# Attention passes of a four-layer graph network: VectorE weighs a batch's rows before it scores the next batch

## The chip, the cores and the metric

The kernel runs on one core of a Trainium2 chip. The metric is device time in microseconds (us) of one execution. Engines are called TensorE (PE; its weight loads are PEld), VectorE (DVE), ScalarE (ACT), GpSimd (POOL) and SyncE (SP). Each has its own instruction queue, taken strictly in order; waits are on semaphores.

## The reference, cut to what matters

The network has 6250 nodes with 256 features and 106250 edges, sorted by target node. Four layers follow one another: a convolution over edges, a mean over neighbours, and two attention layers. The change touches the two attention layers only. With the first three lines ahead of both, they compute (second attention layer, cut; the first has an edge term more in the score, and the second also gives each node a loop to itself):

```
h   = maximum(layernorm(x), 0)
xl  = (h @ W).reshape(n, 8, 32)
a_src, a_dst = einsum('nhc,hc->nh', xl, att_src), einsum('nhc,hc->nh', xl, att_dst)
logits = leaky_relu(a_src[src] + a_dst[dst], 0.2)
ex     = exp(logits - segment_max(logits, dst)[dst])
alpha  = ex / segment_sum(ex, dst)[dst]
out    = segment_sum(xl[src] * alpha[:, :, None], dst).reshape(n, 256) + bias
x      = x + layernorm(out) * gamma + beta
```

## The kernel before, in words

The function gat (L1853) makes one attention pass; it is called twice, with the tags g2 and g3. Edges stand in steps of 128 (one per partition), a step never holds edges of two node tiles of 128 nodes, and 16 steps are a batch: 55 batches a pass (NB). Three buffers of gathered rows (rows0 to rows2) take turns. The helper triples (L96) writes the first three batches out, runs a loop of 17 turns with three batches each, and writes the last batch out.

What happens to batch t:

- GpSimd (gather, L1957) issues 16 indirect DMAs that fetch the sender rows of 16 steps. Ahead of gathers 0, 5, 9 and 14 it waits for marks of other engines (dictionary behind): these are for earlier batches, dt, zt, q1, dt.
- SyncE (load, L1935) loads the indices, the target row numbers (bc), the lines, the heads and in g2 the edge scores.
- VectorE makes the transposed one-hot (transpose_hot, L2100, instruction L2103); TensorE uses it to spread the receivers' scores (spread, L1980, signal sp).
- VectorE scores (score, L2106): it waits for all 16 gathers (gas), for sp and for the turn of the batch before (zt), and adds three terms, L2112, L2114 and L2116. The last gives the signal z.
- TensorE turns the scores (turn, L2005, matmul L2008, signal zt). within (L2118), between (L2138), differ (L2168) and rate (L2162) on VectorE find a running maximum per node and the differences; TensorE turns them back (back, L2019, signal dt), and ScalarE takes the exponent into psT (L2075, L2076, signal w).
- VectorE weighs (weigh, L2181, L2187): it waits for w and multiplies the gathered rows of the batch by the weights in place, in two halves, each with a signal msg.
- TensorE sums the messages per node tile (sums, L1988, matmuls L2001 and L1998), in four quarters of four steps. The first and third quarter wait for a half of msg and for the one-hots sel that ScalarE makes (one_hot, L2052). The quarters use two PSUM buffers in turn.
- VectorE adds the sums to the accumulator (add, L2191, L2203 and L2200), a quarter at a time, and rescales one tile (rescale, L2210, L2214), which also waits for w.

The engines run skewed. VectorE's body(t) handles the differences of batch t, adds the four quarters of batch t - 1, rescales, and then did score(t + 1) and weigh(t). TensorE's body(t) is: tiles_of(t + 1), the four quarters of sums for batch t - 1, factors, back(t), spread(t + 1), turn(t + 1). Both engines begin a body with tiles_of (L1975 and L2217; the calls that show are L1976 and L2218): it loads the numbers of the node tiles of a batch from SBUF into the engine's registers, with one TENSOR_LOAD of 16 or 17 values. There is no planner; the order is the order in which the bodies are written.

Of the kernel before, what the change touches and what calls it, by code (L numbers as in the profile page):

```python
# [164 lines left out]
def wide(t):  # L165
    return t.rearrange("p a d -> p (a d)")
# [1686 lines left out]
def gat(nc, k, tag, edge, own, beta):  # L1853
# [14 lines left out]
    with es:  # L1868
# [214 lines left out]
        def _(v):  # L2083
# [8 lines left out]
            def shifted(t):  # L2092

                x = k.x[:, t * G:(t + 1) * G, :]
                nc.vector.tensor_tensor(x, x, beta_row[:, :].unsqueeze(1).broadcast_to([P, G, D]), ALU.add
                                        ).then_inc(S["xb"], 1)
# [3 lines left out]
            def transpose_hot(t, b, i):  # L2100
                v.wait_ge(S["bc"], t * 16 + 16)
                reach(v, S["sp"], t)
                nc.vector.tensor_scalar(oneT[:, :], bc[:, :], k.lane[:, 0:1], None, ALU.is_equal  # L2103
                                        ).then_inc(S["oh"], 1)

            def score(t, b, i):  # L2106
                v.wait_ge(gas[b], i * full + full)
                v.wait_ge(S["sp"], t + 1)
                reach(v, S["zt"], t)
                a_src = rows[b][:, :, 0:TW].rearrange("p u (h c) -> p h u c", c=HW)[:, :, :, CH]  # L2110
                part = psE[:, 0:U * 3 * H].rearrange("p (u q h) -> p q h u", q=3, h=H)
                nc.vector.tensor_tensor(z[:, :, :], a_src, part[:, 0], ALU.add).then_inc(S["v"], 1)  # L2112
                v.wait_ge(S["v"], t * 13 + 1)
                nc.vector.tensor_tensor(z[:, :, :], z[:, :, :], part[:, 1], ALU.add).then_inc(S["v"], 1)  # L2114
                v.wait_ge(S["v"], t * 13 + 2)
                nc.vector.tensor_tensor(z[:, :, :], z[:, :, :], part[:, 2], ALU.add).then_inc(S["z"], 1)  # L2116

            def within(t, b, i):  # L2118
                v.wait_ge(S["zt"], t + 1)
                v.wait_ge(lns[b], i * 16 + 16)  # L2120
                useless = k.mask[:, ds(t, 1)]
                if edge:
                    v.wait_ge(aes[b], i * 16 + 16)
                    nc.vector.scalar_tensor_tensor(out=zz[:, :], in0=psE[:, scores], scalar=useless, in1=ae[b][:, :],
                                                   op0=ALU.add, op1=ALU.add).then_inc(S["v"], 1)
                else:
                    nc.vector.tensor_scalar(zz[:, :], psE[:, scores], useless, None, ALU.add).then_inc(S["v"], 1)
                v.wait_ge(S["v"], t * 13 + 3)
                nc.vector.scalar_tensor_tensor(out=sc[:, :], in0=zz[:, :], scalar=0.2, in1=zz[:, :], op0=ALU.mult,
                                               op1=ALU.max).then_inc(S["v"], 1)  # L2130
                v.wait_ge(S["v"], t * 13 + 4)
                nc.vector.tensor_tensor_scan(fwd[:, :], ln[b][:, pen], sc[:, :], LOW, ALU.add, ALU.max
                                             ).then_inc(S["v"], 1)
                v.wait_ge(S["v"], t * 13 + 5)
                nc.vector.tensor_tensor_scan(loc[:, ::-1], ln[b][:, nextp][:, ::-1], fwd[:, ::-1], LOW, ALU.add, ALU.max
                                             ).then_inc(S["loc"], 1)
# [31 lines left out]
            def differ(t, b, i):  # L2168
                v.wait_ge(S["v"], t * 13 + 12)
                reach(v, S["dt"], t)  # L2170
                nc.vector.scalar_tensor_tensor(out=m1[:, :], in0=ln[b][:, pref], scalar=cf[:, 0:1], in1=loc[:, :],
                                               op0=ALU.add, op1=ALU.max).then_inc(S["v"], 1)
                v.wait_ge(S["v"], t * 13 + 13)
                nc.vector.scalar_tensor_tensor(out=mx[:, :], in0=ln[b][:, suf], scalar=cb[:, 0:1], in1=m1[:, :],
                                               op0=ALU.add, op1=ALU.max).then_inc(S["mx"], 1)
                v.wait_ge(S["mx"], t + 1)
                if own:
                    nc.vector.tensor_tensor(me[:, :], ln[b][:, last], mx[:, :], ALU.mult)
                nc.vector.tensor_tensor(df[:, :], sc[:, :], mx[:, :], ALU.subtract).then_inc(S["d"], 1)

            def weigh(t, b, i):  # L2181
                v.wait_ge(S["w"], t + 1)
                weight = psT[:, turned].rearrange("p (h u) -> p u h", h=H)
                for half in range(2):
                    u = slice(half * (U // 2), (half + 1) * (U // 2))
                    r = rows[b][:, u, 0:TW].rearrange("p u (h c) -> p u h c", c=HW)
                    nc.vector.tensor_tensor(r[:, :, :, 0:CH], r[:, :, :, 0:CH],  # L2187
                                            weight[:, u, :].unsqueeze(3).broadcast_to([P, U // 2, H, CH]), ALU.mult
                                            ).then_inc(S["msg"], 1)

            def add(t, at, q):  # L2191

                summed(v, t, q)
                of = psA[:, q % 2]
                for n in range(Q):
                    u = q * Q + n
                    ready = known(v, t * U + u if u else t + 1)
                    to = wide(k.acc[:, ds(at[u], 1), :])
                    if n == 3:
                        ins = nc.vector.tensor_tensor(to, to, of[:, 2, 0:RW], ALU.add)  # L2200
                    else:
                        to = to.rearrange("p (o d) -> p o d", o=2)
                        ins = nc.vector.tensor_tensor(to, to, of[:, 0:2, n * HALF:(n + 1) * HALF], ALU.add)  # L2203
                    if u:
                        ins._wait_ge(S["acc"], ready)
                    else:
                        ins._wait_ge(S["rs"], ready)
                    ins.then_inc(S["acc"], 1)

            def rescale(t, at):  # L2210
                v.wait_ge(S["w"], t + 1)
                v.wait_ge(S["acc"], t * U)
                to = wide(k.acc[:, ds(at[U], 1), 0:TW]).rearrange("p (h c) -> p h c", c=HW)
                nc.vector.scalar_tensor_tensor(out=to, in0=psT[:, factor].unsqueeze(2).broadcast_to([P, H, HW]),  # L2214
                                               scalar=1.0, in1=to, op0=ALU.add, op1=ALU.mult).then_inc(S["rs"], 1)

            def tiles_of(t):  # L2217
                return nc.values_load_multi_w_load_instructions(  # L2218
                    k.node_of[0:1, ds(t * KP, K)], engines=[DVE], min_val=0, max_val=NT - 1,
                    skip_runtime_bounds_check_because="made in prepare() from counts of at most NT - 1")[1]  # L2220

            def body(t, b, i):
                first = isinstance(t, int) and t == 0
                last_one = isinstance(t, int) and t == NB - 1
                after, more = (b + 1) % 3, i + (b + 1) // 3
                if first:
                    transpose_hot(0, 0, 0)
                    for n in range(5):
                        shifted(n)
                    score(0, 0, 0)  # L2230
                else:
                    at = tiles_of(t - 1)
                    if isinstance(t, int) and t <= 2:
                        shifted(t + 4)
                if not last_one:
                    transpose_hot(t + 1, after, more)
                within(t, b, i)
                if not first:
                    add(t - 1, at, 0)
                between(t, b, i)  # L2240
                if not first:
                    add(t - 1, at, 1)
                differ(t, b, i)
                rate(t, b, i)
                if first:
                    v.sem_inc(S["rs"], 1)
                else:
                    add(t - 1, at, 2)
                    add(t - 1, at, 3)
                    rescale(t, at)  # L2250
                if not last_one:
                    score(t + 1, after, more)
                weigh(t, b, i)

            triples(v, NB, body)
            at = tiles_of(NB - 1)
            for q in range(4):
# [316 lines left out]
```

## Time and profile before

| | us |
|---|---|
| median of 3 runs | 5556.87 (5554.14 to 5564.05) |
| profiled execution | 5560.9 |
| its span | 5559.1 |
| VectorE busy in the span | 4053.2 (73%) |
| TensorE busy | 3861.1 (69%) |
| GpSimd busy | 3637.7 (65%) |
| ScalarE busy | 2944.2 (53%) |

The span is the time from the first to the last recorded instruction. The shares are means over the four layers and what lies between. The attention passes take about 2940 to 4107 us (g2) and 4283 to 5453 us (g3) of the span. "Idle before" an instruction is the time its engine stood still ahead of it, with what ended that; "issue" means that the profile shows nothing that was waited for. The instructions of a queue's sequencer (PEldq, DVEq: register operations, semaphore waits) are not counted as busy. The granted clock is a share of TensorE's full 2.4 GHz.

### The profile page before, as it was taken

Reading aid. Unit: us, or ns where it says so; the run is one execution under the profiler, and the core shown is the slowest. Engines: PE = TensorE matmul, PEld = TensorE weight load, DVE = VectorE, ACT = ScalarE, POOL = GpSimd, SP = SyncE. Lnnn points to the kernel's source line nnn. Section 1 sums busy time; section 2 is a strip of 40 time slices with the busy share of each in tenths; the row PEclk is TensorE's granted clock in tenths of the full one; section 3 lists DMA queues with packets and bytes.
Section 4 is the critical chain, followed back from the end, with each engine's and each line's share of the span. In section 5 each row is a group of like instructions: output and inputs, shape, how many; then the busy total and the mean of one; then the engine's idle time right before and its main releaser. Section 6 shows DMA issues by size and latency. Waiting matters only on the chain. (4 is left out here: it accounts for less than half of the span.)

```text
span 5559.1 us, 88639 instructions
## 1 busy us (share of the span) xinstructions
PE 3861.1 (69%) x21123; PEld 3024.9 (54%) x21124; DVE 4053.2 (73%) x9127; ACT 2944.2 (53%) x8412; POOL 3637.7 (65%) x3635
## 2 busy tenths in 40 slices
PE   4799999999775666666674555555565555665565
PEld 3577777777554555555553455444533445555552
DVE  4799999999773333333376888887876788888888
ACT  4799999999554444444453333333334334333432
POOL 2577777777327777777706777777721777777770
PEclk9999999999877888888786777777787777777777
DMA  8444444444215544555435555555522555554542
GB/s 265 116 97 99 98 99 99 98 99 98 68 60 140 134 134 133 134 134 134 116 121 153 146 146 146 144 143 145 146 87 79 141 140 144 144 144 142 141 138 95
DMA packets 705680, 700.27 MB, mean 126 GB/s; under 512 B 458546, under 2 KB 574063, under 8 KB 703779
## 3 DMA queue, kind: packets, MB, share of 16 engines
q0 software_dynamic: 173552, 491.76, 31.2%
q1 hardware_dynamic: 390663, 177.29, 12.4%
q10 hardware_dynamic: 141372, 30.14, 2.8%
q8 instruction: 39, 0.64, 0.0%
q14 instruction: 54, 0.44, 0.0%
HBM read 634.29 MB, written 64.08 MB: 126 GB/s over the span
## 5 line engine op out<-in xcount | busy, mean ns | idle before, releaser
L1135 POOL DMA_INDIRECT c0rows<-rows,c0idx x872 | 986.6, 1131 | 282.8 <-issue 268.2
L1967 POOL DMA_INDIRECT g2rows<-sender_rows,g2idx x864 | 844.0, 977 | 264.8 <-issue 259.8
L1967 POOL DMA_INDIRECT g3rows<-sender_rows,g3idx x864 | 829.4, 960 | 281.3 <-issue 261.6
L901 POOL DMA_INDIRECT g1rows<-rows,g1idx x872 | 833.5, 956 | 265.7 <-issue 260.5
L1022 DVE TENSOR_TENSOR acc<-acc,g1psA 128x258 f32 x660 | 279.9, 424 | 725.2 <-PE g1psA L927 569.7
L1164 ACT ACTIVATE c0z<-c0rows,c0sh 128x128 f32<-128x128 f32 x2640 | 795.7, 408 | 1.6 <-DVE c0prod L1331 1.6
L930 PE MATMUL g1psA<-g1rows,g1sel 128*128 128x129 f32 x2640 | 475.3, 348 | 360.3 <-DMA g1rows<-rows,g1idx 317.3
L930 PEld LDWEIGHTS g1psA<-g1rows,g1sel 128*128 128x128 f32 x2640 | 456.2, 259 | 403.3 <-issue 339.2
L2001 PE MATMUL g3psA<-g3rows,g3sel 128*128 128x136 f32 x2640 | 444.2, 328 | 156.8 <-DVE g3rows L2187 102.5
L1256 PE MATMUL c0psA<-c0prod,c0sel 128*128 128x256 f32 x1760 | 547.2, 393 | 3.5 <-DVE acc L1345 3.5
L2001 PE MATMUL g2psA<-g2rows,g2sel 128*128 128x132 f32 x2640 | 432.7, 324 | 165.0 <-DVE g2rows L2187 102.4
L2001 PEld LDWEIGHTS g3psA<-g3rows,g3sel 128*128 128x128 f32 x2640 | 412.3, 231 | 231.4 <-issue 113.1
L2001 PEld LDWEIGHTS g2psA<-g2rows,g2sel 128*128 128x128 f32 x2640 | 401.9, 231 | 236.8 <-issue 113.3
L1259 PE MATMUL c0psA<-c0prod,c0sel 128*128 128x192 f32 x1760 | 430.3, 326 | 0.0
L1345 DVE TENSOR_TENSOR acc<-acc,c0psA 128x256 f32 x880 | 367.7, 418 | 24.7 <-PE c0psA L1259 2.1
L955 ACT ACTIVATE g1fT<-g1psF 128x512 f32<-128x512 f32 x104 | 62.1, 597 | 574.9 <-PE g1psA L927 574.9
L1259 PEld LDWEIGHTS c0psA<-c0prod,c0sel 128*128 128x128 f32 x1760 | 334.8, 190 | 45.7
L1256 PEld LDWEIGHTS c0psA<-c0prod,c0sel 128*128 128x128 f32 x1760 | 298.6, 190 | 76.5 <-DVE acc L1345 65.3
L2203 DVE TENSOR_TENSOR acc<-acc,g3psA 128x272 f32 x660 | 286.2, 434 | 19.7 <-PE g3psA L1998 2.5
L2203 DVE TENSOR_TENSOR acc<-acc,g2psA 128x264 f32 x660 | 280.8, 425 | 19.5 <-PE g2psA L1998 2.4
L2069 ACT ACTIVATE g2al<-g2arg 128x2 f32<-128x2 f32 x55 | 11.2, 203 | 512.2 <-DVE g2arg L2159 477.3
L970 ACT ACTIVATE g1sel<-iota,dst_in 128x128 f32<-128x128 f32 x880 | 267.7, 389 | 9.3 <-PEq L80 5.1
(445 smaller groups left out, 8725.0 us busy)
## 6 DMA issues: line engine op xcount, KB each, us to landing
g2bc<-dst_rows SPq DMA_DIRECT2D x55, 512.0 KB, 3.9
g3bc<-dst_rows SPq DMA_DIRECT2D x55, 512.0 KB, 3.9
g1f<-in_edge_attr SPq DMA_DIRECT2D x103, 256.0 KB, 3.5
c0rows<-rows,c0idx POOLq DMA_INDIRECT x872, 2.8
g1rows<-rows,g1idx POOLq DMA_INDIRECT x872
g2rows<-sender_rows,g2idx POOLq DMA_INDIRECT x864
g3rows<-sender_rows,g3idx POOLq DMA_INDIRECT x864
rbf_steps<-prep_extra POOLq DMA_DIRECT2D x7, 1024.0 KB, 11.1
```

The lines of the kernel that those rows point to most:

```text
L901: g.indirect_dma_start(rows[b][:, u, 0:D], None, k.table, bass.IndirectOffsetOnAxis(ap=at[:, u:u + 1], axis=0)).then_inc(r_sem[b], 16)
L930: ins = nc.tensor.matmul(to[:, o, n * HALF:(n + 1) * HALF], sel[b][:, u, :], rows[b][:, u, o * HALF:(o + 1) * HALF], start=True, stop=True)
L970: ins = nc.scalar.activation(sel[b][:, u, :], k.iota[:, :], ACT.Abs, bias=k.dst_in[:, ds(t * U2 + u, 1)], scale=-1.0)
L1022: ins = nc.vector.tensor_tensor(to, to, of[:, 0:2, n * HALF:(n + 1) * HALF], ALU.add)
L1135: g.indirect_dma_start(rows[b][:, m, place(n), :], None, k.table, bass.IndirectOffsetOnAxis(ap=at[:, 4 * m + n:4 * m + n + 1], axis=0)).th ...
L1164: ins = nc.scalar.activation(z[:, m, place(n), 1 + x:5 + x:3, :], row[:, 0:2 + x:1 + x, :], ACT.Copy, scale=sh[b][:, 4 * m + n, 1 + x:2 + x])
L1256: nc.tensor.matmul(out, sel[b][:, 4 * m + n, :], prod[:, m, 0, place(n), :, :].rearrange("p k c -> p (k c)"), start=True, stop=False)
L1259: ins = nc.tensor.matmul(out[:, C:], sel[b][:, 4 * m + n, :], prod[:, m, 1, place(n), 1:4, :].rearrange("p k c -> p (k c)"), start=False, ...
L1345: ins = nc.vector.tensor_tensor(to, to, psA[:, q, u, :], ALU.add)
L1967: g.indirect_dma_start(rows[b][:, u, 0:TW], None, k.sender_rows, bass.IndirectOffsetOnAxis(ap=at[:, u:u + 1], axis=0)).then_inc(gas[b], 16)
L2001: ins = nc.tensor.matmul(to[:, o, n * HALF:(n + 1) * HALF], sel[:, u, :], rows[b][:, u, o * HALF:(o + 1) * HALF], start=True, stop=True)
L2203: ins = nc.vector.tensor_tensor(to, to, of[:, 0:2, n * HALF:(n + 1) * HALF], ALU.add)
```

## The change

In VectorE's body, weigh(t) moves from behind score(t + 1) to ahead of it. Nothing else changes.

```diff
@@ -2248,9 +2248,9 @@
                     add(t - 1, at, 2)
                     add(t - 1, at, 3)
                     rescale(t, at)
+                weigh(t, b, i)
                 if not last_one:
                     score(t + 1, after, more)
-                weigh(t, b, i)
 
             triples(v, NB, body)
             at = tiles_of(NB - 1)
```

## Rows read from the trace of the kernel before

**Rows 1.** Grouped lines, VectorE's first score instruction: count, busy, mean ns, idle before.

```profile
L2112 DVE TENSOR_TENSOR g2z<-g2rows,g2psE 128x128 f32<-128x128 f32 x55 | 21.1, 383 | 175.8 <-DMA g2rows<-sender_rows,g2idx 175.1 <-DMA g2rows<-sender_rows,src_of 0.7
L2112 DVE TENSOR_TENSOR g3z<-g3rows,g3psE 128x128 f32<-128x128 f32 x55 | 20.2, 368 | 160.0 <-DMA g3rows<-sender_rows,g3idx 159.2 <-DMA g3rows<-sender_rows,src_of 0.8
```

**Rows 2.** The same line: ns min/median/max, first and last start; part and whole pass.

```profile
L2112 DVE TENSOR_TENSOR g2z<-g2rows,g2psE x23: 382/383/386, 3501.1 to 3951.6; 128x128 f32<-128x128 f32 x23
L2112 DVE TENSOR_TENSOR g3z<-g3rows,g3psE x23: 366/368/373, 4518.3 to 4968.9; 128x128 f32<-128x128 f32 x23
...
L2112 DVE TENSOR_TENSOR g2z<-g2rows,g2psE x55: 380/383/386, 2965.6 to 4075.6; 128x128 f32<-128x128 f32 x55
L2112 DVE TENSOR_TENSOR g3z<-g3rows,g3psE x55: 365/368/373, 4308.5 to 5420.3; 128x128 f32<-128x128 f32 x55
```

**Rows 3.** Timeline of GpSimd: start, duration, what, idle before; g2, then g3.

```profile
3526.16 0.96 POOL L1967 DMA_INDIRECT g2rows<-sender_rows,g2idx  x1 [0.30 <-issue]
3527.42 1.02 POOL L1967 DMA_INDIRECT g2rows<-sender_rows,g2idx  x1 [0.30 <-issue]
...
4712.59 0.94 POOL L1967 DMA_INDIRECT g3rows<-sender_rows,g3idx  x1 [0.63 <-issue]
```

**Rows 4.** Timeline of VectorE, one batch of g2.

```profile
3501.09 0.38 DVE L2112 TENSOR_TENSOR g2z<-g2rows,g2psE 128x128 f32<-128x128 f32 x1 [3.00 <-DMA g2rows<-sender_rows,g2idx]
...
3502.04 4.48 DVE L2187 TENSOR_TENSOR g2rows<-g2rows,g2psT 128x2048 f32<-128x2048 f32 x2
3506.43 0.75 DVE L2103 TENSOR_SCALAR g2oneT<-g2bc,lane 128x2048 bf16<-128x2048 bf16 x1
...
3508.60 1.33 DVE L2203 TENSOR_TENSOR acc<-acc,g2psA 128x264 f32 x3
...
3518.14 0.43 DVE L2214 SCALAR_TENSOR_TENSOR acc<-g2psT,acc 128x264 f32 x1 [0.23 <-DVE acc L2200]
3521.51 0.38 DVE L2112 TENSOR_TENSOR g2z<-g2rows,g2psE 128x128 f32<-128x128 f32 x1 [2.94 <-DMA g2rows<-sender_rows,g2idx]
```

**Rows 5.** Timeline of TensorE, the same batch: turn, first and second quarter.

```profile
3502.17 0.47 PE L2008 MATMUL g2psE<-ident,g2z 128*128 128x128 f32 x1 [5.73 <-DVE g2z L2116]
3504.45 3.00 PE L2001 MATMUL g2psA<-g2rows,g2sel 128*128 128x132 f32 x12 [1.81 <-DVE g2rows L2187]
...
3508.13 1.64 PE L2001 MATMUL g2psA<-g2rows,g2sel 128*128 128x132 f32 x12
```

**Rows 6.** Sequencer operations by line, ns min/median/max, starts: all, then single batches.

```profile
L1976 PEldq TENSOR_LOAD <-node_of x110: 1102/1107/1287, 2954.3 to 5400.0; - x110
L2218 DVEq TENSOR_LOAD <-node_of x110: 1335/1344/1365, 2987.5 to 5437.3; - x110
...
L1976 PEldq TENSOR_LOAD <-node_of x1: 1107/1107/1107, 3502.3 to 3502.3; - x1
L1976 PEldq TENSOR_LOAD <-node_of x1: 1103/1103/1103, 3523.1 to 3523.1; - x1
L153 PEldq FUSED_REGOPS  x1: 42/42/42, 3504.4 to 3504.4; - x1
```

**Rows 7.** Busy time by window: PE, PEld, DVE, ACT, POOL, granted clock, DMA share, GB/s.

```profile
3508.09:3508.59 0.50, 0.50 (x4) 0.46 (x3) 0.47 (x2) 0.00 (x0) 0.28 (x1) 0.72 0.00 0
```

**Rows 8.** Timeline of VectorE, then TensorE, at the last batch of g2.

```profile
4092.07 0.43 DVE L2214 SCALAR_TENSOR_TENSOR acc<-g2psT,acc 128x264 f32 x1 [0.22 <-DVE acc L2200]
4092.41 4.47 DVE L2187 TENSOR_TENSOR g2rows<-g2rows,g2psT 128x2048 f32<-128x2048 f32 x2
4098.78 1.36 DVE L2203 TENSOR_TENSOR acc<-acc,g2psA 128x264 f32 x3 [1.89 <-PE g2psA L1998]
...
4094.75 3.01 PE L2001 MATMUL g2psA<-g2rows,g2sel 128*128 128x132 f32 x12 [5.13 <-DVE g2rows L2187]
```

**Rows 9.** Timeline of VectorE in one batch of g3: first add, rescale.

```profile
4914.82 1.38 DVE L2203 TENSOR_TENSOR acc<-acc,g3psA 128x272 f32 x3
...
4924.70 0.43 DVE L2214 SCALAR_TENSOR_TENSOR acc<-g3psT,acc 128x264 f32 x1 [0.23 <-DVE acc L2200]
```

## The prediction

> **What bounds the kernel now.** Only the two attention passes (tags g2 and g3, 55 batches each) run the edited code, so I read those stretches alone. The grouped lines come first: VectorE's first score instruction (L2112) is preceded by 175.8 us of idle time in g2, nearly all ended by the DMA that gathers the rows, 3.2 us a batch [rows 1]. On that view the change looks like a plain gain: 4.4 us of weighing could go into a 3 us hole. The distance between score instructions is the second thing to see: 450.5 us over 22 batches, 20.48 us, in both passes [rows 2]. Third, GpSimd: it issues sixteen gathers a batch, each 0.96 us with 0.30 us between ("issue"), so 20.2 us at the least; one or two a batch are stretched to 1.02 and more, and in g3 the tenth gather waits 0.63 instead of 0.30 us, for its pacing wait on TensorE's second quarter of sums (L1998) [rows 3]. So the period is GpSimd's: g2 20.45 us from its own instructions, g3 20.15 plus 0.33 of that wait. VectorE's hole is slack, and filling it can return at most g3's 0.33 us a batch.
>
> **What the loop through VectorE and TensorE becomes.** What matters then is whether the new order's own loop still fits in 20.48 us. I call the start of L2112 Z and take the timeline of one g2 batch [rows 4, 5]. Now: Z 3501.09; first weigh 3502.04 (Z+0.95); transposed one-hot 3506.43, so two weighs cost 4.39; first add 3508.60 (Z+7.51); rescale 3518.14, that is 9.54 after the first add, nearly all busy; then 2.94 idle to the next Z. TensorE: turn (L2008, 0.47 us) at 3502.17 (Z+1.08), first sums at 3504.45 (Z+3.36), set off by the first weigh half, second quarter 3.68 us later.
>
> After the change the weighs start right behind the rescale: 0.34 us behind its start, as in the last batch, where that order exists already [rows 8]. Z is 4.39 after that, if the gather is there. No wait is new for weigh: rescale waits for the same weights (S["w"]).
>
> The sums no longer wait for a weigh, they stand behind the turn in TensorE's queue, but not directly. Between turn(t+1) and sums(t, 0) the next body begins, with tiles_of: a TENSOR_LOAD that brings 16 tile numbers into TensorE's registers, 1.107 us, 110 times [rows 6]. It starts at 3502.3 when Z is 3501.09 (Z+1.2), and at 3523.1 when Z is 3521.51 (Z+1.6) in every third batch, where the loop's branch comes first [rows 4, 6]. Today it is hidden: it ends at Z+2.3 or Z+2.7, and the weigh half arrives at Z+3.3. With the weighs done earlier it is on the path. Behind it come the waits for the one-hots and for the messages with their register operations, each 32 to 51 ns plus dispatch; the last one stands at 3504.4, just ahead of the sums [rows 5, 6]. I take 0.3 us for them (estimate from those rows; between 0.1 and 0.5). So the sums start at Z+2.6 in two batches of three and Z+3.0 in the third, 2.75 on the mean, not at Z+1.56 where the turn ends. VectorE has such a load too, 1.344 us [rows 6], hidden behind the weighs today and bare behind the score then: its one-hot starts near Z+2.4 (2.85 with the branch) instead of Z+0.95; adding the 2.17 from there to the first add gives Z+4.6, earlier than the sums deliver, so it costs nothing unless the sums get faster by 2 us.
>
> From the first sums to the first add where VectorE waits for them: 4.03 us, from the last batch (4094.75 to 4098.78) [rows 8]. It contains a quarter at the granted clock 0.50 (1.2 GHz), which TensorE has after its idle time; the clock rises to full about 3.9 us after the sums begin, within the half microsecond from 3508.09 [rows 5, 7]. The cover that hid this quarter was the second weigh half plus one-hot plus within, 5 us of VectorE work; it shrinks to one-hot and within, about 2.8. That is the new stall: VectorE waits about 2 us for the first quarter instead of 3 us for the gather, and this wait lies in the loop.
>
> Loop in g2: 2.75 + 4.03 + 9.54 + 0.34 + 4.39 = 21.05 us. In g3 the first add comes at 4914.82 and the rescale at 4924.70, 9.88 us for the wider rows [rows 9]: 21.39 us. Both exceed 20.48. GpSimd is then no longer the bound; its three pacing waits are met earlier or at the same place relative to Z (turn Z+1.5 as now; second quarter about Z+8.5, from where seven gathers and the landing, 8.5 + 0.3 + 2.0 us, reach Z+19.4). SyncE's loads of the one-hot row, the lines and the heads follow the one-hot and the difference step, both earlier relative to the next Z, so they are covered. ScalarE's one-hots for the sums end before the weighs do. The moved step issues no DMA of its own.
>
> **Sum.** From first to last Z g2 takes 1110.0 us and g3 1111.8 [rows 2]. After: three batches written out ahead of the loop, where TensorE waits as now for slow gathers, about 64.2 us, and 51 intervals of 21.05 (1073.6) or 21.39 (1090.9): 1137.8 and 1155.1, that is +28 and +43. I round the pair up by 4, since in the loop a register operation lies between the quarter's signal and the first add that the written-out last batch does not show. In the last body there is no tiles_of on TensorE, so its first sums come at Z+1.6 rather than at 3.3: -1.3 us a pass, -3 in all. Together +72 on the profiled execution's 5560.9 (span 5559.1): 5633. The median of the runs shown is 4 us lower, 5556.87, so 5629.
>
> The Trainium skill, page "DMA: Bandwidth & Descriptors", section "Latency and other measured facts", gives a tensor_load a floor of about 600 ns. The trace has 1.107 us for TensorE's, so it doesn't agree for this 16-register load. By the page's figure the sums would start at Z+2.2, the loops be 20.5 and 20.85, and the kernel would take about 5577 (an estimate from that figure).
>
> Another possible price is GpSimd. A gather beside VectorE's bf16 one-hot took 1.02 us instead of 0.96 [rows 3]; the one-hot moves to other gathers but stays one a batch. Bounds: 0.06 us off, or the whole one-hot (0.66 us) added to a gather. GpSimd has 0.6 us a batch to spare in the new loop, so I take 0. The Trainium skill, page "SBUF — State Buffer", section "Who interferes with whom", has GpSimd fully blocked during such an operation; the trace shows a small part of that, and by the full block GpSimd would need about 20.8 us, still just under the new loops.
>
> **Rivals.**
> A, forecast: the register load and the cold quarter enter the loop, 21.05 and 21.4 us a batch, 5629. Chance 0.80.
> B, faster: the load is hidden after all (fetched while the turn waits for z), and the sums start at Z+1.56. Loops of 19.9 and 20.2 fit; g2 falls back on GpSimd's 20.45, g3 loses its 0.33 us wait less a little, 0.25 x 52 = 13, first batches and ends give 6: 5538. For it: the load touches no operand of the turn. Against it: it is seen at Z+1.2 in each batch, always after the turn is released. Chance 0.08. It decides from sums before Z+2.15.
> C, no change: half of the load hidden, loops of 20.45 to 20.5, within 11 us: 5557. Chance 0.07.
> D, worse: the sums keep their Z+3.36, since something else (the queue's other waits) holds them: loops of 21.66 and 22.0, 1.2 x 52 + 1.5 x 52 = 140, about 5695. For it: no batch of the loop shows the sums starting without a weigh to wait for. Against: today's start follows the end of the first weigh half (Z+0.95 and half of 4.39) within 0.3 us [rows 4, 5]. Chance 0.05.
>
> **Numbers.** About 0.2% (11 us) is what a measurement can tell from no change. Slower holds A and D, 0.85; same 0.07; faster 0.08. The range: A alone is uncertain by the 0.2 of the waits, 0.1 of the quarter, and the clock, whose rise need not keep its 3.9 us behind the start of the sums (I allow 0.9 us earlier or 2 later, -0.4 to +0.3 us a batch); together 0.4 x 104, so 5587 to 5672. I take 5585 to 5680.
>
> **What would show it.** Right: L2112 idle almost gone, and most of it now before the first add (L2203), about 2 us, released by TensorE's L1998; sums 2.6 to 3.0 us behind Z with the TENSOR_LOAD just before; GpSimd gaps over 0.30 us at the gathers 6, 10 or 15; periods 21.0 and 21.4. Wrong: L2112 still waiting for the gather with 20.4 us periods (B or C), or sums at Z+1.6; or gathers well over 1.0 us in all batches, which would make it GpSimd's.

## The result, and the profile after

| | before | after |
|---|---|---|
| median | 5557.85 us (4 runs) | 5628.38 us (4 runs, 5625.33 to 5631.00) |
| profiled execution, span | 5560.9, 5559.1 | 5625.33, 5623.5 |

The ratio is 1.0127, 95% interval 1.0113 to 1.0141: slower by 1.3%. The forecast was 5629. The medians lie 70.5 us apart, and the interval allows 63 to 78.

The grouped lines of the kernel after answer to [rows 1 and 3]: VectorE's first score instruction, the adds of the first three steps of a quarter, and the gathers (busy, mean ns | idle before, what ended it).

```profile
L1967 POOL DMA_INDIRECT g3rows<-sender_rows,g3idx x864 | 833.7, 965 | 320.3 <-issue 231.0 <-PE g3psA L1998 71.1 <-PE g3psT L2023 9.4
L2203 DVE TENSOR_TENSOR acc<-acc,g3psA 128x272 f32 x660 | 287.7, 436 | 122.8 <-PE g3psA L1998 105.5
L2203 DVE TENSOR_TENSOR acc<-acc,g2psA 128x264 f32 x660 | 282.2, 428 | 119.2 <-PE g2psA L1998 101.9
L2103 DVE TENSOR_SCALAR g2oneT<-g2bc,lane 128x2048 bf16<-128x2048 bf16 x55 | 42.2, 767 | 77.8 <-issue 77.7
L2112 DVE TENSOR_TENSOR g2z<-g2rows,g2psE 128x128 f32<-128x128 f32 x55 | 20.8, 378 | 13.0 <-DMA g2rows<-sender_rows,g2idx 12.3 <-DMA g2rows<-sender_rows,src_of 0.8
```

The wait for the gather is gone, 13 us in g2 where it was 175.8, as the change means to have it. In its place stand two new ones: 101.9 us in g2 ahead of the first add, until TensorE has summed the first quarter (L1998), and 77.8 us ahead of the one-hot, while VectorE loads its registers (1.34 us a batch). GpSimd now has idle time behind TensorE's sums, 71.1 us in g3: it has stopped being the bound.

First and last start of the score (to be held against [rows 2]) give the length of each pass.

```profile
L2112 DVE TENSOR_TENSOR g2z<-g2rows,g2psE x55: 373/379/385, 2962.5 to 4098.7; 128x128 f32<-128x128 f32 x55
L2112 DVE TENSOR_TENSOR g3z<-g3rows,g3psE x55: 358/363/373, 4329.7 to 5485.5; 128x128 f32<-128x128 f32 x55
```

g2 went from 1110.0 to 1136.2 us, g3 from 1111.8 to 1155.8: 26 and 44 us, 70 in all, where the two profiled executions differ by 64. Of the 6 us, 3.0 are given back between the last score and the last add of the two passes, and 3.1 lie ahead of g2's first score (2965.6 before, 2962.5 after), where the change does nothing.

One batch of g2 in the timeline of the kernel after, VectorE, then TensorE (compare [rows 4, 5]), with the start of TensorE's register load in the line's own view (compare [rows 6]):

```profile
3526.87 0.43 DVE L2214 SCALAR_TENSOR_TENSOR acc<-g2psT,acc 128x264 f32 x1 [0.23 <-DVE acc L2200]
3527.22 4.48 DVE L2187 TENSOR_TENSOR g2rows<-g2rows,g2psT 128x2048 f32<-128x2048 f32 x2
3531.61 0.38 DVE L2112 TENSOR_TENSOR g2z<-g2rows,g2psE 128x128 f32<-128x128 f32 x1
...
3534.45 0.75 DVE L2103 TENSOR_SCALAR g2oneT<-g2bc,lane 128x2048 bf16<-128x2048 bf16 x1 [1.82 <-issue]
...
3538.69 1.36 DVE L2203 TENSOR_TENSOR acc<-acc,g2psA 128x264 f32 x3 [1.98 <-PE g2psA L1998]
```

```profile
3532.69 0.47 PE L2008 MATMUL g2psE<-ident,g2z 128*128 128x128 f32 x1 [7.04 <-DVE g2z L2116]
3534.65 3.00 PE L2001 MATMUL g2psA<-g2rows,g2sel 128*128 128x132 f32 x12 [1.49 <-issue]
...
3538.33 1.84 PE L2001 MATMUL g2psA<-g2rows,g2sel 128*128 128x132 f32 x12
```

```profile
L1976 PEldq TENSOR_LOAD <-node_of x1: 1105/1105/1105, 3533.2 to 3533.2; - x1
```

Z is 3531.61, with no idle time ahead of it. The turn starts at Z+1.08, the load at 3533.2 (Z+1.6, this is a batch with the loop's branch) and runs to 3534.3, and the sums start at 3534.65, Z+3.04. Most of the 1.49 us of "issue" in that row is the load: the profile's releasers know only semaphores, so a register load shows as idle time for which nothing is to blame. The first add comes at 3538.69, 4.04 us behind the sums.

### The profile page after: what moved, and what is told of

It reads as the page before. It is cut to its first block and busy times, and to the rows that moved or that the text cites. A ratio compares the mean times of both kernels' runs of the same rounds, so it can differ in the third digit from the quotient of the medians.

```text
span 5623.5 us, 88639 instructions
## 1 busy us (share of the span) xinstructions
PE 3872.0 (69%) x21123; PEld 3058.6 (54%) x21124; DVE 4066.4 (72%) x9127; ACT 2944.8 (52%) x8412; POOL 3641.0 (65%) x3635
## 5 line engine op out<-in xcount | busy, mean ns | idle before, releaser
L2001 PE MATMUL g3psA<-g3rows,g3sel 128*128 128x136 f32 x2640 | 459.7, 337 | 107.0 <-issue 64.2
L2001 PEld LDWEIGHTS g3psA<-g3rows,g3sel 128*128 128x128 f32 x2640 | 430.7, 240 | 171.4 <-issue 80.7
L2001 PE MATMUL g2psA<-g2rows,g2sel 128*128 128x132 f32 x2640 | 451.0, 335 | 105.5 <-issue 63.8
L2001 PEld LDWEIGHTS g2psA<-g2rows,g2sel 128*128 128x128 f32 x2640 | 424.5, 242 | 166.9 <-issue 80.5
L2203 DVE TENSOR_TENSOR acc<-acc,g2psA 128x264 f32 x660 | 282.2, 428 | 119.2 <-PE g2psA L1998 101.9
L2008 PE MATMUL g3psE<-ident,g3z 128*128 128x128 f32 x55 | 26.1, 475 | 396.4 <-DVE g3z L2116 396.4
L2008 PE MATMUL g2psE<-ident,g2z 128*128 128x128 f32 x55 | 26.1, 475 | 395.8 <-DVE g2z L2116 395.8
```

What stands on the lines that cost most here:

```text
L2001: ins = nc.tensor.matmul(to[:, o, n * HALF:(n + 1) * HALF], sel[:, u, :], rows[b][:, u, o * HALF:(o + 1) * HALF], start=True, stop=True)
```

## The experiments

Each ran on the same chip as runs of the kernel before; the ratios are against those. "Z+..." are means over the batches of the loop in g2. Three theories are named in the expectations: P says that GpSimd's gathers set the pace since the one-hot slows them, V that VectorE's register load does, and A is the account of the forecast.

**Moving the register load.** In TensorE's body:

```diff
-                if not last_one:
-                    at = tiles_of(t + 1)
...
                     sums(t - 1, before, 2).then_inc(S["q2"], 1)
-                    sums(t - 1, before, 3)
+                if not last_one:
+                    at = tiles_of(t + 1)
+                if not first:
+                    sums(t - 1, before, 3)
```

On the kernel after (a_pe_early): 

> The kernel after, with TensorE's tiles_of(t + 1) moved from the head of its body to between the third and fourth quarter of the sums, where TensorE stands idle 0.8 us. Theory A (TensorE's register load lies between turn and sums, in the loop): the sums start at Z+1.9 instead of Z+2.6 or 3.0, loops of 20.3 (then GpSimd's 20.45 decides) and 20.6 us, so 5628 falls by about 70, to 5558. Theory V (the price is VectorE's own register load, bare behind the score): unchanged, 5628. Theory P (gathers slowed by the one-hot at its new place): unchanged, 5628.

Measured: 5540.79 us, 0.9976 (0.9966 to 0.9985), 17 us lower than I expected. On the kernel before (b_pe_early): 

> The kernel before with the same move of TensorE's tiles_of. Theory A: the load was hidden there by the wait for the first weigh half, so no change, 5557 within 6. V and P say the same. If it were faster by 20 us or more, the load had a price before the change too and the account of A is incomplete.

Measured: 5554.66 us, 0.9998 (0.9989 to 1.0007). The same edit is worth nothing in the old order and 88 us in the new one. TensorE in the first of the two, one batch:

```profile
3521.06 0.48 PE L2008 MATMUL g2psE<-ident,g2z 128*128 128x128 f32 x1 [7.86 <-DVE g2z L2117]
3521.74 3.00 PE L2001 MATMUL g2psA<-g2rows,g2sel 128*128 128x132 f32 x12 [0.20 <-issue]
```

The sums start 0.7 us behind the turn (Z+1.5 on the mean, I had expected Z+1.9), and g3 takes 1100.5 us. That is less than before the change: the second quarter is summed earlier, so the tenth gather no longer waits for it (0.30 us ahead of it, where it was 0.64 on the mean). V and P are out as the main cause. The turned order with this one move is better than the kernel before.

**Doubling the loads.** The first try (a_pe_double) called tiles_of twice and used only the second result. 

> The kernel after with TensorE's tiles_of(t + 1) done twice in a row at the head of its body. Theory A: each batch is longer by one more load, 1.11 us plus about 0.05, in 2 x 51 intervals: +118, 5746. Theories V and P: TensorE has idle time elsewhere, no change, 5628.

Measured: 5624.65 us, 1.0124 (1.0109 to 1.0140). That would speak against A, but the line's own view shows that nothing was doubled:

```profile
L1976 PEldq TENSOR_LOAD <-node_of x110: 1102/1106/1287, 2954.2 to 5468.3; - x110
```

110 loads, as ever: the second load, whose registers nobody reads, does not show in the trace, so this run is no test of A but a repeat of the kernel after. The second try uses half of each:

```diff
-                    at = tiles_of(t + 1)
+                    more = tiles_of(t + 1)
+                    at = [*tiles_of(t + 1)[:8], *more[8:]]
```

On TensorE (a_pe_double2): 

> The kernel after with two register loads at the head of TensorE's body, half of the tile numbers used from each, so that both stay in the program. Theory A (TensorE's load lies in the loop between turn and sums): the sums start at Z+3.9 instead of 2.77, 1.15 us more in each of 2 x 51 intervals, +117: 5745. Theory V (VectorE's load sets the pace) and theory P (GpSimd does): no change, 5628.

Measured: 5745.92 us, 1.0346 (1.0331 to 1.0362), 117.5 us above the kernel after. The load's count, and the starts of the sums of a batch whose Z is 3534.40:

```profile
L1976 PEldq TENSOR_LOAD <-node_of x218: 1100/1104/1292, 2947.6 to 5581.6; - x109
```

```profile
3538.20 3.00 PE L2001 MATMUL g2psA<-g2rows,g2sel 128*128 128x132 f32 x12 [2.25 <-issue]
```

The same on VectorE's tiles_of(t - 1) (a_dve_double2): 

> The kernel after with two register loads at the head of VectorE's body, both in use. Theory A: VectorE's one-hot moves from Z+2.5 to Z+3.9 and within ends at Z+6.0, still before the first quarter is summed at Z+6.7, so 5628 within 12. Theory V: 1.35 us more in 2 x 51 intervals, +138: 5766. Theory P: between, as the one-hot meets other gathers, at most +0.4 us a batch, 5670.

Measured: 5625.11 us, 1.0127 (1.0112 to 1.0143), the time of the kernel after. The one-hot comes 1.4 us later (Z+3.9) and the wait ahead of the first add shrinks by as much. One engine's load costs its full length a batch (117.5 us in 102 intervals, 1.15 us each), the other's nothing: the loop runs through TensorE's queue there.

**The low clock.** Idle matmuls ahead of the turn, 16 and then 28 (nobody reads their results):

```diff
             def turn(t):
+                reach(pe, S["acc"], (t - 1) * U - Q)
+                for _n in range(28):
+                    nc.tensor.matmul(psA[:, 0, 2, 0:P], k.ident[:, :], k.ident[:, :], start=True, stop=True)
                 pe.wait_ge(S["z"], t + 1)
                 reach(pe, S["loc"], t)
```

> The kernel after with 16 more matmuls of 128 x 128 on the identity, written to an unused part of the sums' PSUM and never read, in TensorE's idle time between spread and turn. Theory A's second term (the first quarter runs at 1.2 GHz since TensorE stood idle before it): the clock stays high, the quarter takes 2.1 instead of 3.7 us, the first add comes at Z+5.1 instead of 6.75, loops of 19.4 and 19.8 us, under GpSimd's 20.5 and 20.3: 5540. If the clock has no part in it: 5628, or more if the matmuls delay the turn.

Measured: 5607.73 us, 1.0098 (1.0083 to 1.0114). 

> The kernel after with 28 idle matmuls ahead of the turn. The 16 of the earlier run took 3.8 us and left 3.3 us of idle time before the turn, the granted clock was 0.5 in most first quarters again, and the time 5607. 28 should take 6.7 us of the 7.1 there. Theory A: no low clock at the sums, the quarter takes 2.1 us instead of 3.7, loops of 19.5 and 19.8 fit under GpSimd's 20.5 and 20.3: 5545. If the first quarter stays at 3.7 us or the time at 5607 or over, the low clock is not what costs there, or the added work delays the turn.

Measured: 5555.55 us, 0.9992 (0.9983 to 1.0002). TensorE in one batch of the second:

```profile
3502.44 0.33 PE L2011 MATMUL g2psE<-ident,g2z 128*128 128x128 f32 x1 [2.06 <-DVE g2z L2119]
3503.91 1.59 PE L2001 MATMUL g2psA<-g2rows,g2sel 128*128 128x132 f32 x12 [1.15 <-issue]
```

The twelve matmuls take 1.59 us instead of 3.00. By windows (PE, PEld, DVE, ACT, POOL busy, granted clock, DMA share, GB/s), first of this run, then of the kernel after:

```profile
3000.00:4070.00 1070.00, 897.97 (x6859) 815.72 (x6858) 867.44 (x2081) 403.10 (x1091) 815.67 (x834) 0.94 0.51 143
```

```profile
3000.00:4070.00 1070.00, 617.44 (x3864) 537.70 (x3865) 846.12 (x2035) 392.69 (x1061) 792.78 (x815) 0.74 0.51 141
```

16 matmuls did not do it, and my expectation of 5540 failed by 68 us: they ended 2.9 to 4.6 us before the turn, and in 87 of the loop's 102 intervals the first quarter still took more than 3.5 us. With 28 the granted clock is 0.94 of full in the pass, not 1; the quarter takes 2.0 to 2.1 us in 59 of the 102, more than 3.5 in 22 and something between in 21: 10 us short of what I expected, but 73 below the kernel after. This shows the second term of the loop too, the quarter at 1.2 GHz.

**The gathers and the one-hot.** Only one half of the weighing goes ahead (the edit is against the kernel after; weigh takes the halves that it is to do as its last argument, that part is left out):

```diff
-                if not last_one:
-                    score(t + 1, after, more)
-                weigh(t, b, i)
+                weigh(t, b, i, (0,))
+                if not last_one:
+                    score(t + 1, after, more)
+                weigh(t, b, i, (1,))
```

(b_half) 

> The kernel before with only the first weigh half moved ahead of the score; the second stays behind it. Theory A: the first half (2.2 us) fits into the 3 us wait for the gather, the second half still covers the register loads and the cold quarter, the sums start at Z+2.6 to 3.0 and the first add comes at about Z+6.9 instead of 7.5; the loop is 19 us, so GpSimd bounds both passes: g2 20.45 us, g3 20.2 (its tenth gather waits less, as the second quarter comes 0.6 us earlier): 5540. Theory P: the one-hot is back at its old place, so 5557. Theory V: VectorE's load is hidden again, 5540 to 5557.

Measured: 5576.27 us, 1.0037 (1.0023 to 1.0051). My expectation of 5540 failed by 36 us, on the wrong side of the kernel before. VectorE's one-hot and two gathers of one batch:

```profile
3529.38 0.74 DVE L2103 TENSOR_SCALAR g2oneT<-g2bc,lane 128x2048 bf16<-128x2048 bf16 x1
```

```profile
3529.52 1.43 POOL L1967 DMA_INDIRECT g2rows<-sender_rows,g2idx  x1 [0.30 <-issue]
3531.26 1.13 POOL L1967 DMA_INDIRECT g2rows<-sender_rows,g2idx  x1 [0.30 <-issue]
```

A gather that starts 0.14 us into the one-hot takes 1.43 instead of 0.96 us: 0.47 us more, where 0.60 of the one-hot are left. The fifth gather does so in nearly every batch (1.39 us on the mean in g2). GpSimd, still the bound in that order, needs 20.8 us. The test is to move the one-hot alone:

```diff
+                within(t, b, i)
                 if not last_one:
                     transpose_hot(t + 1, after, more)
-                within(t, b, i)
```

(b_half_hot) 

> The kernel with one weigh half ahead of the score (the earlier run that took 5576), and the transposed one-hot moved behind within. Theory P, now with a size: in that run the one-hot started at Z+3.14 and the fifth gather, due at Z+3.4 while it ran, took 0.43 us longer, so GpSimd needed 20.8. Behind within it starts at about Z+4.7, just behind the start of a gather at Z+4.64 and over before the next at Z+5.9: stretches of 0.2 us or less in a batch, g2 20.4, g3 20.2, 5540. If the stretch isn't due to where the one-hot meets the gathers, 5576 stays.

Measured: 5553.49 us, 0.9999 (0.9990 to 1.0008). From 5576 down by 23, and 13 above what I expected. Gathers over 1.0 us in the batches past the third of g2 went from 106 to 4. What is left shows in the grouped lines, first without, then with this move:

```profile
L1967 POOL DMA_INDIRECT g2rows<-sender_rows,g2idx x864 | 861.2, 997 | 264.4 <-issue 251.2 <-PE g2psT L2023 10.1 <-PE g2psA L1998 2.7
```

```profile
L1967 POOL DMA_INDIRECT g2rows<-sender_rows,g2idx x864 | 830.9, 962 | 276.8 <-issue 264.6 <-PE g2psA L1998 11.6 <-PE g2psE L2008 0.3
```

30 us less of gathering in g2, 12 us more of waiting, ahead of the tenth gather and for the second quarter of the sums (0.57 us of idle time there on the mean, 0.32 without the move). Adding TensorE's register load in its early place (b_all): 

> The kernel with one weigh half ahead of the score, the one-hot behind within, and TensorE's register load between the third and fourth quarter. Theory A: the sums start at Z+1.5, the loop is under 18 us in both passes, and the second quarter is ready 1.3 us earlier, so the tenth gather's extra wait (1.52 and 1.62 us from gather to gather in the run without this last edit) goes. GpSimd's own sixteen gathers are left, 20.25 us in g2 and 20.05 in g3: 5521. If the tenth gather's wait has another cause, 5553 stays.

Measured: 5524.10 us, 0.9933 (0.9919 to 0.9946): the fastest version. Its gathers and score:

```profile
L1967 POOL DMA_INDIRECT g2rows<-sender_rows,g2idx x864 | 831.9, 963 | 263.2 <-issue 256.8 <-PE g2psA L1998 5.8 <-PE g2psT L2023 0.3
L2113 DVE TENSOR_TENSOR g2z<-g2rows,g2psE 128x128 f32<-128x128 f32 x55 | 21.0, 382 | 150.7 <-DMA g2rows<-sender_rows,g2idx 150.0 <-DMA g2rows<-sender_rows,src_of 0.7
```

Sixteen bare gathers a batch bound both passes (20.22 and 20.04 us), and VectorE is back to waiting 2.7 us a batch for them, which is slack.

The same two moves on the kernel after (a_pe_early_hot): 

> The kernel after with TensorE's register load between the third and fourth quarter (the run that took 5541) and the one-hot behind within, near Z+4.0. Theory P: fewer stretched gathers, GpSimd at 20.25 us in g2 instead of 20.5, and in g3 the loop's 20.2: 5527. If the stretches there don't depend on the one-hot: 5541.

Measured: 5546.21 us, 0.9973 (0.9962 to 0.9984): no better than without the second move, and my expectation failed by 19 us. There the loop is about as long as the gathers (g3 20.36 us), and the one-hot does not stay at one place between them: in g2 it starts at Z+3.96 to Z+4.60, in b_half_hot at Z+4.64 to Z+4.67. The fourth to sixth gather shared the stretches. In b_half_hot most one-hots start 0.0 to 0.1 us behind the start of a gather, which keeps its 0.96 us; here most start 0.6 to 0.7 us behind one, and nearly a third at 1.2, just ahead of the next. The aim at a gap between two gathers held where the gathers release the score.

**What held g3 before.** The kernel before with one wait less:

```diff
-                behind = {0: (S["dt"], t - 1), 5: (S["zt"], t), 9: (S["q1"], t - 1), 14: (S["dt"], t)}
+                behind = {0: (S["dt"], t - 1), 5: (S["zt"], t), 14: (S["dt"], t)}
```

> The kernel before without GpSimd's wait ahead of the tenth gather. Reading of the profile of before: g3 loses its 0.33 us a batch (20.15 us instead of 20.48) and g2 0.02: 5555 minus 18, 5537. If the period of 20.48 has another cause in g3, the time moves to another gather or to the landing, 5555.

Measured: 5549.72 us, 0.9980 (0.9971 to 0.9989), 10 us below the kernel before where I expected 18. g3 goes from 1111.8 to 1099.1 us, 0.24 us a batch of the 0.33 that stood at the tenth gather, g2 stays: the reading holds, with a tenth of a microsecond a batch given back in stretched gathers (965 ns on the mean in g3 instead of 960).

## Why the prediction was right

It named the outcome, the place and the mechanism, and the medians' difference was forecast as 72 us and measured as 70.5. That the last figure came out within 1 us of the median is luck: the interval is 15 us wide, and between the profiled executions it was 64 us against the same 72. Point by point:

- The bound. GpSimd's gathers set the 20.48 us in both passes and VectorE's 3 us hole was slack [rows 1 to 3]. Right: removing the hole (13 us of idle time left in g2) gained nothing, and b_no_gate9 moved g3 alone. This is the step that kept the forecast from being the plain "3.2 us times 110".
- The start of the sums. Forecast Z+2.75 on the mean, measured Z+2.77 in g2 and Z+2.76 in g3. That the load would be bare rested on its starts in [rows 6]; moved away it gives the time back, doubled it takes 117.5 us (forecast there 117).
- The first quarter. Forecast 4.03 us to the first add, from the last batch [rows 8]; measured 3.97 in g2 and 4.05 in g3. What its low clock costs is shown by a_warm28.
- The loops. Forecast 21.05 and 21.39 us, measured 21.00 and 21.41. VectorE's wait of about 2 us for the quarter: 1.9.
- VectorE's own load costs nothing: right, by a_dve_double2.
- The ends, -3 us in all: -2.0 in g2 and -1.0 in g3 from the last score to the last add. The term was put together loosely: Z+1.6 instead of Z+3.3 makes 1.7 us a pass and not 1.3, and measured was Z+1.4 instead of Z+3.3.
- The 4 us that I added for a register operation ahead of the first add were not there. The sum came out at 5633 for the profiled execution and 5625 was measured: these 4 us too many, and 3.1 us by which the profiled kernel after was ahead before the first pass began. At the medians the miss does not show, since the profiled run of the kernel after was the fastest of its four, 3 us below their median.

Two details were wrong without weight in the sum. GpSimd's gaps were expected at the gathers 6, 10 or 15; in the loop's batches those beyond 0.4 us are all at the tenth, up to 2.4 us in g2 and 3.1 in g3. They are longest where the second quarter of the sums took over 2.8 us instead of about 2.0: 1.33 us on the mean there in g2 and 2.50 in g3, 0.67 and 1.02 in the other batches. And I read [rows 3] as if the one-hot could stretch a gather by little: 1.02 instead of 0.96 us was a gather that began near the one-hot's end. b_half shows most of the rest of the one-hot (0.47 of 0.60 us). The Trainium skill ("SBUF — State Buffer", section "Who interferes with whom") says that GpSimd is fully blocked while such an operation of VectorE runs, if VectorE was first; the trace agrees with that but for 0.13 us. In the kernel after the loop had 0.6 us a batch to spare over the gathers in g2 (sixteen times 0.975 and 0.30 us make 20.4 of 21.0), and that made the misreading cheap. In b_half, where GpSimd is the bound, it cost 23 us.

For a tensor_load the Trainium skill ("DMA: Bandwidth & Descriptors", section "Latency and other measured facts") gives a floor of about 600 ns. These runs show 1.10 us for 16 values on TensorE, in every run: that lies above the floor, so it does not contradict it, though the prediction says that the two disagree; it only shows that the floor is not the price of this load.

Rivals: B (load hidden) is what a_pe_early builds by hand, 5541 against its 5538. C and D did not occur.

A second gather, that no longer overlaps the one-hot, takes 1.13 us too (row at 3531.26). The traces settle what holds it: the second of the two scans in within (L2135), which reads two tensors in SBUF. Two batches of b_half in g3, and the last batch of g2 in the kernel before, in which SyncE has no load left to issue:

```profile
4659.62 0.50 DVE L2135 TENSOR_TENSOR_SCAN g3loc<-g3ln,g3fwd 128x128 f32<-128x128 bf16 x1
4659.66 0.94 POOL L1967 DMA_INDIRECT g3rows<-sender_rows,g3idx  x1 [0.30 <-issue]
...
4680.18 0.42 DVE L2135 TENSOR_TENSOR_SCAN g3loc<-g3ln,g3fwd 128x128 f32<-128x128 bf16 x1
4680.23 1.14 POOL L1967 DMA_INDIRECT g3rows<-sender_rows,g3idx  x1 [0.30 <-issue]
...
4061.28 0.42 DVE L2135 TENSOR_TENSOR_SCAN g2loc<-g2ln,g2fwd 128x128 f32<-128x128 bf16 x1
4061.34 1.14 POOL L1967 DMA_INDIRECT g2rows<-sender_rows,g2idx  x1 [0.30 <-issue]
```

Either the gather is held or the scan is. A gather that the one-hot stretched puts the start of the next one some 0.05 us behind that of the scan. Over the two kernels and the twelve runs, from the third batch of each pass on and without those beside the one-hot, that happened 775 times. Every gather recorded 46 ns or more behind the scan took 1.12 us or more, beside a scan of 0.42; every one at 43 ns or less kept its 0.94 to 0.96 us, and the scan took 0.49 to 0.50. In b_half_hot the one-hot holds almost no gather, so almost none starts at that place, and both stretches go together. SyncE's loads are not the cause: in b_half_hot no gather that met only them took over 1.0 us.

What stays open: why 22 first quarters of a_warm28 still ran at the low clock.

## What to carry to other kernels

An idle gap on a busy engine is no gain in store: find who sets the period first, then add up the loop that the new order makes, with every operation of each queue on it. Register loads and other sequencer work don't count as busy and show as "issue"; ahead of a reorder look at what lies between two instructions in the queue, since the wait that is removed may be what hid it. Work that fills a gap should be only as much as the gap holds, here half of the weighing, and what moves with it (the one-hot) should be laid just behind the start of a transfer that it would block.

## What the runs showed of the hardware that I had not expected

- A gather (indirect DMA from GpSimd) that starts 0.14 us into VectorE's comparison of 2048 bf16 values takes 1.43 us instead of 0.96 (b_half). With the comparison placed just behind a gather's start it stays at 0.96 (b_half_hot): 30 us less of gathering in g2, of which the loop got back 0.36 us a batch.
- A VectorE scan over two tensors in SBUF (L2135) and a gather hold each other up too: a gather recorded 46 ns or more behind the scan takes 0.18 us longer, and beside one at 43 ns or less it is the scan that takes 0.07 us longer.
- A register load whose result is not used did not show in the trace at all (a_pe_double). No run shows where it was dropped.
- The idle time just ahead of an instruction did not decide TensorE's clock. In a_warm the turn came after 2.9 to 4.6 us of idle time and still ran at full clock (0.33 us instead of 0.47) in 62 of 102 intervals, with a quarter of over 3.5 us behind it in 47 of these. In a_warm28, with 0.4 to 2.2 us of idle time, it did so in 101 of 102, and 22 quarters were slow.
